# Layer normalisation with a centring product, squares read from PSUM and scaling on VectorE

## What is computed

```python
def _ln_t(v, eps=1e-05):
    m = jnp.mean(v, axis=-1, keepdims=True)
    s = jnp.var(v, axis=-1, keepdims=True)
    return (v - m) / jnp.sqrt(s + eps)
...
x = _L0_conv_ref(x, ...)
t = _to_tokens(x)
t = t + _L1_attn_ref(_ln_t(t), ...)
t = t + _L1_ffn_ref(_ln_t(t), ...)
x = _from_tokens(t, x)
```

## Time and profile before

| What | Value |
|---|---|
| Median of 3 runs | 844.76 us (843.91 to 859.37) |
| The profiled execution: its own time | 852.07 us |
| Its span, first to last instruction | 850.1 us |
| Mean granted TensorE clock | 0.83 |
| Busy: TensorE, VectorE, ScalarE, GpSimd | 688.6, 444.9, 414.2, 132.5 us |
| The attention's normalisation lies at | 513.7 to 540.2 us |
| The experts' normalisation lies at | 783.4 to about 804 us |

### The profile page before, as it was taken

The page is one execution under the profiler, slowest core; times in us unless marked ns, Lnnn a source line. Parts: engine busy times, 40 slices in busy tenths (PEclk is TensorE's granted clock), DMA queues, the critical chain, the costliest instruction groups (busy, mean ns, idle before and its releaser), DMA issues.

```text
span 850.1 us, 42114 instructions
## 1 busy us (share of the span) xinstructions
PE 688.6 (81%) x19610; PEld 502.1 (59%) x19610; DVE 444.9 (52%) x797; ACT 414.2 (49%) x819; POOL 132.5 (16%) x215
## 2 busy tenths in 40 slices
PE   6787777888768789787788675889999999998546
PEld 2355555556552356565566464668888888886333
DVE  0574545445440564545545547246666666664654
ACT  1665554644412665454644414245556665564532
POOL 7000000000003000000000001333444444431400
PEclk8989788876767897778976956559999999999669
DMA  6400000000000400000000005300000000000002
GB/s 179 86 5 4 5 5 5 4 4 5 5 5 5 85 4 5 4 5 5 4 5 5 4 5 123 106 2 2 1 0 0 0 0 0 0 0 2 0 2 99
DMA packets 7691, 16.60 MB, mean 20 GB/s; under 512 B 1837, under 2 KB 5805, under 8 KB 7141
## 3 DMA queue, kind: packets, MB, share of 16 engines
q1 hardware_dynamic: 7534, 14.21, 6.7%
HBM read 10.34 MB, written 3.87 MB: 17 GB/s over the span
## 4 chain that ended last, share of the span: by engine, by line
PE 74%; issue 11%; ACT 6%; DVE 5%; DMA 1%; POOL 1%; SPq 0%; ACTq 0%; DVEq 0%
PE banks L227 21%; PE banks L145 14%; PE banks L716 8%; PE banks L693 4%; PE banks L760 4%; PE banks L458 4%; PE banks L741 4%; PE banks L775 4%; PE banks L180 2%; PE banks L166 2%; ACT hx L273 1%; PE banks L706 1%; ACT hy L278 1%; DVE norm_stats L629 1%; PE banks L729 1%
## 5 line engine op out<-in xcount | busy, mean ns | idle before, releaser
L227 PE MATMUL banks<-s,y 32*64 32x96 f32 (+9 forms) x10752 | 196.1, 271 | 70.8 <-issue 70.5
L318 DVE TENSOR_TENSOR s<-hy,hx 128x384 f32<-128x384 f32 (+3 forms) x336 | 144.6, 476 | 189.1 <-PE banks L227 187.0
L227 PEld LDWEIGHTS banks<-s,y 32*64 32x64 f32 x10752 | 164.0, 157 | 116.2 <-issue 106.3
L145 PE MATMUL banks<-w_dc,tiled 64*32 64x192 f32 x3584 | 128.2, 412 | 19.2 <-issue 12.9
L268 ACT COPY y<-banks 128x384 f32<-128x384 f32 x192 | 81.7, 484 | 108.8 <-PE banks L145 108.6
L145 PEld LDWEIGHTS banks<-w_dc,tiled 64*32 64x32 f32 x3584 | 74.4, 131 | 51.3 <-issue 24.1
L278 ACT ACTIVATE hy<-banks 128x512 f32<-128x512 f32 (+2 forms) x144 | 72.9, 584 | 44.4 <-PE banks L180 44.3
L273 ACT ACTIVATE hx<-banks 128x384 f32<-128x384 f32 x144 | 61.3, 504 | 34.8 <-PE banks L166 28.4
L957 POOL TENSOR_TENSOR y<-y,stats 128x1024 f32<-128x1024 f32 x32 | 60.8, 1901 | 109.3 <-DVE stats L889 109.2
L879 DVE TENSOR_REDUCE stats<-banks 128x16 f32<-128x1024 f32 x32 | 39.2, 1225 | 69.6 <-PE banks L716 69.6
L716 PEld LDWEIGHTS banks<-src,y 64*128 64x128 f32 x1024 | 64.5, 201 | 7.9 <-issue 7.9
(11 more groups left out here) (134 smaller groups left out, 737.4 us busy)
## 6 DMA issues: line engine op xcount, KB each, us to landing
src<-in_x_dram SPq DMA_DIRECT2D x4, 578.0 KB, 5.5
y<-in_w_dram SPq DMA_DIRECT2D x1, 2080.0 KB
off<-in_w_dram SPq DMA_DIRECT2D x2, 1024.0 KB
out_dram<-tokens SPq DMA_DIRECT2D x4, 512.0 KB, 2.6
offsets_dram<-tokens SPq DMA_DIRECT2D x32, 54.0 KB
off<-offsets_dram SPq DMA_DIRECT2D x16, 108.0 KB
w_dc<-in_w_dc_dram SPq DMA_DIRECT2D x2, 288.0 KB, 6.4
y<-in_w_attn_dram SPq DMA_DIRECT2D x1, 512.0 KB, 5.0
```

What stands on the lines that cost most here:

```text
L145: last = nc.tensor.matmul(m.ps[32 * j:32 * j + 32, FIRST_BANK + (count + g) % RING, (col % 2) * 192:(col % 2) * 192 + 192], m.tiled[rows, ...
L227: last = nc.tensor.matmul(out[:, r0:r0 + strip.n, first:first + width], m.y[32 * j:32 * j + 32, g, (s // 3) % 2 * Y_SLOTS + strip.slot, co ...
L318: nc.vector.tensor_tensor(dst, hy, hx[:, :, r0:r0 + strip.n, :], ALU.mult).then_inc(cv.s_ready, 1)
```

## The change

The turn and the centring become one operation. A constant 128 by 128 matrix `centring` (identity less 1/64 within each image's 64 channels) is loaded, and the 8 transpositions of a pair become 8 products with it as the moving operand, so that PSUM holds centred tokens. `centre` on VectorE goes (three instructions a pair). ScalarE squares straight from PSUM. The multiplication moves from GpSimd to VectorE (`scale`), which reads PSUM and writes `xt`; `norm_pool` goes. A product into banks that an earlier pair used now waits for that pair's `scale`. TensorE's program becomes: products 0 and 1, then product 2, back 0, product 3, back 1, back 2, back 3. VectorE's becomes: variance 0 and 1, and then for each pair its invert, its scale and the variance two pairs on. ScalarE's keeps its order.

```diff
+    def centre(pr):
...
         if pr >= 2:
-            pe.wait_ge(ln.centred, pr - 1)
+            pe.wait_ge(ln.scaled, pr - 1)
         for b in range(PIX // P):
-            last = nc.tensor.transpose(m.ps[:, 4 * (pr % 2) + b // 4, b % 4 * P:(b % 4 + 1) * P],
-                                       m.tokens[:, pr, b * P:(b + 1) * P], m.identity[:, :])
-        last.then_inc(ln.turned, 1)
+            last = nc.tensor.matmul(m.ps[:, 4 * (pr % 2) + b // 4, b % 4 * P:(b % 4 + 1) * P],
+                                    m.tokens[:, pr, b * P:(b + 1) * P], m.centring[:, :], start=True, stop=True,
+                                    skip_group_check=True)
+        last.then_inc(ln.centred, 1)
...
+    centre(0)
+    centre(1)
+    for pr in range(PAIRS):
+        if pr + 2 < PAIRS:
+            centre(pr + 2)
+        back(pr)
...
-        nc.scalar.activation(ln.square[:, pr % 2, :, :], ln.xt[pr], ACT.Square).then_inc(ln.squared, 1)
+        nc.scalar.activation(ln.square[:, pr % 2, :, :].rearrange("p b n -> p (b n)"),
+                             m.ps[:, 4 * (pr % 2):4 * (pr % 2) + 2, :].rearrange("p a n -> p (a n)"), ACT.Square
+                             ).then_inc(ln.squared, 1)
...
+    def scale(pr):
+        centred = m.ps[:, 4 * (pr % 2):4 * (pr % 2) + 2, :].rearrange("p a n -> p (a n)").rearrange(
+            "p (b a c) -> p b a c", a=2, c=C)
+        dve.wait_ge(ln.rstd_ready, pr + 1)
+        nc.vector.tensor_tensor(ln.xt[pr].rearrange("p b (a c) -> p b a c", a=2), centred,
+                                over_channels(ln.rstd[:, pr, :]), ALU.mult).then_inc(ln.scaled, 1)
+
+    variance(0)
+    variance(1)
     for pr in range(PAIRS):
-        if pr + 1 < PAIRS:
-            centre(pr + 1)
-        if pr:
-            invert(pr - 1)
-        variance(pr)
-    invert(PAIRS - 1)
+        invert(pr)
+        scale(pr)
+        if pr + 2 < PAIRS:
+            variance(pr + 2)
...
-        pe.wait_ge(ex.ln.centred, 3 + group)
+        pe.wait_ge(ex.ln.scaled, 3 + group)
...
+    c["centring"] = (np.eye(P) - np.kron(np.eye(2), np.ones((C, C))) / C).astype(f32)
```

More of the change, by code:

```diff
@@ L569, in norm_pe @@
 def norm_pe(nc, pe, m, ln, beside):
-    for pr in range(PAIRS):
+    def centre(pr):
         if ("turn", pr) in beside:
@@ L575, in norm_pe, with back @@
         if pr >= 2:
-            pe.wait_ge(ln.centred, pr - 1)
+            pe.wait_ge(ln.scaled, pr - 1)
         for b in range(PIX // P):
-            last = nc.tensor.transpose(m.ps[:, 4 * (pr % 2) + b // 4, b % 4 * P:(b % 4 + 1) * P],
-                                       m.tokens[:, pr, b * P:(b + 1) * P], m.identity[:, :])
-        last.then_inc(ln.turned, 1)
-    for pr in range(PAIRS):
+            last = nc.tensor.matmul(m.ps[:, 4 * (pr % 2) + b // 4, b % 4 * P:(b % 4 + 1) * P],
+                                    m.tokens[:, pr, b * P:(b + 1) * P], m.centring[:, :], start=True, stop=True,
+                                    skip_group_check=True)
+        last.then_inc(ln.centred, 1)
+    def back(pr):
         if ("back", pr) in beside:
@@ L623, in over_channels @@
         return stat.rearrange("p (b a) -> p b a", a=2).unsqueeze(3).to_broadcast([P, PIX // P, 2, C])
[L625 to L636, removed]
     def variance(pr):
@@ L646, in invert @@
         nc.vector.reciprocal(ln.rstd[:, pr, :], ln.rstd[:, pr, :]).then_inc(ln.rstd_ready, 1)
-    centre(0)
-    for pr in range(PAIRS):
-        if pr + 1 < PAIRS:
-            centre(pr + 1)
-        if pr:
-            invert(pr - 1)
-        variance(pr)
-    invert(PAIRS - 1)
[L658 to L663, removed]
+    def scale(pr):
[6 more added lines that the diff above has]
+    variance(1)
+    for pr in range(PAIRS):
+        invert(pr)
+        scale(pr)
+        if pr + 2 < PAIRS:
+            variance(pr + 2)
 TURN_AHEAD, KEYS_AHEAD, SCORES_AHEAD, QUERIES_AHEAD = 1, 2, 3, 4
@@ L1167, in program @@
         m.identity = sb("identity", [P, P])
+        m.centring = sb("centring", [P, P])
         m.tiled = sb("tiled", [P, PAIRS, TR, TC, TILE_ROWS * TILE_COLS])
@@ L1289, in program @@
         ex.ln.xt = [ex.xt[:, :, pr, :] for pr in range(PAIRS)]
-        norm_stats = sb("norm_stats", [P, 3, PAIRS, STATS])
+        norm_stats = sb("norm_stats", [P, 2, PAIRS, STATS])
         for ln in (at.ln, ex.ln):
-            ln.mean, ln.squares, ln.rstd = (norm_stats[:, k, :, :] for k in range(3))
+            ln.squares, ln.rstd = (norm_stats[:, k, :, :] for k in range(2))
             ln.square = s_all[:, 1024:3072].rearrange("p (s b n) -> p s b n", s=2, n=P)
@@ L1296, in program @@
             ln.tokens_before = PAIRS if ln is at.ln else 0
-            ln.turned = sem(name + "_turned")
-            ln.summed = sem(name + "_summed")
-            ln.mean_ready = sem(name + "_mean_ready")
             ln.centred = sem(name + "_centred")
@@ L1391, in program @@
             conv1_loads.append((off_buffer.bitcast(U16)[32 * rg + ROW_COORD:32 * rg + ROW_ONE + 1, :], a["places"][rg]))
-        loads = [(m.identity[:, :], a["identity"]),
+        loads = [(m.identity[:, :], a["identity"]), (m.centring[:, :], a["centring"]),
                  (convs[1].w_off[:, :, :], a["w_off2"]), (convs[1].w_dc[:, :, :], a["w_dc2"]),
@@ L1439, in _ @@
             pool.wait_ge(cleared, PAIRS)
-            norm_pool(nc, pool, m, at.ln)
             attention_pool(nc, pool, m, at)
             pool.wait_ge(at.added, 2 + ALL_BLOCKS)
-            norm_pool(nc, pool, m, ex.ln)
             pool.wait_ge(ex.ln.scaled, PAIRS)
```

## The result

The changed kernel runs in 851.83 us, median of 11 executions (846.47 to 857.75). The kernel before, measured beside it, has 848.96 us (837.25 to 859.37, 11 executions). The ratio is 1.0089, with a 95% interval of 1.0055 to 1.0123: 0.9% slower. Ratios in this document leave out executions more than 1.5% above the fastest of their kernel (here five of the eleven before and none of the changed kernel), and since this program's executions spread that far by themselves, medians over all of them stand beside the ratios. Over all executions the medians differ by 2.9 us and the means (849.6 and 852.4) by 2.8, with a standard error of 2.2 worked out from the 22 times. So the whole times alone say that the change is worth little, and leave its sign open; that has to be read from the stages.

A forecast was written before the change was run, and what follows sets the result against it. It took chains of waits to bound the normalisations, mostly VectorE's sums and subtractions in the experts'. Attention's +1.6 and experts' +4 gave +5.6 us on a median of 844.8, rounded to 851, range 841 to 858.

The forecast's parts named there:

- Twice the records: Centring on TensorE: a pair takes 16 records where there were 8, 1.97 us at the high clock and 3.7 low.
- One chain instead of two pairs in flight: Both normalisations: product 2 waits for scale 0, scale 1 comes after it; 7.55 us per step low clock, 5.82 high.
- two ahead: Engine order: variance and square of pair 2 stand ahead of reciprocal and root of pair 1.
- The rival that the pairs run beside each other: Both normalisations: scale 1 follows scale 0 by VectorE's 2.7 us a pair, saving some 5 us each; 835 us; 3%.
- Scale 0: First pair's multiplication, now on VectorE: ends at 523.95 in the attention's normalisation and 791.6 in the experts'.
- early lead over GpSimd's multiplication: Attention's normalisation: scale 0 ends at 523.95 instead of 527.8 on GpSimd, 3.8 us ahead, given back afterwards.
- +1.6 forecast: Attention's normalisation: 1.6 us longer, taken as the middle between low and high clock throughout.
- the ends of -0.8 and +4.0: Attention's normalisation: 0.8 us earlier with the high clock throughout, 4.0 us later with the low clock throughout.
- +3 forecast for the chain: Experts' normalisation: first gate product 3 us later, between 0.8 at the high clock and 5.1 at the low.
- The further +1 for the gate products: After the experts' normalisation: 1 us more, since at the low level the gate products' 1.89 us become up to 3.8.
- The rival of a clock held high through the opening: Normalisations and attention's opening: centring bursts keep the clock high, sum -5 us, 840 us; 14%.
- the prediction's third sign of being wrong: Attention's opening: the prediction is wrong if it runs at another clock than before.

The follow-up runs named there:

- experiment with turns: Changed kernel with the 8 centring products of a pair made transpositions with the identity again, mean not subtracted; median 846.62 us against 846.27 before, ratio 1.0003.
- second changed execution: The changed kernel profiled once more without any edit; 844.93 us in a single execution, beside 855.05 us for the kernel before.
- own banks: Changed kernel with two PSUM banks for each of the four pairs and all four products first on TensorE; ratios to the kernel before 0.9793 and 0.9805.

## Why the prediction was right

**The time.** 851 was forecast, 851.83 measured, in the range, and the direction was forecast too (5.6 us slower; the ratio says 0.9%, some 7.5 us; the medians differ by 2.9; the two stages by 5.3). That the forecast hit the median so closely is luck: the median of before was given as 844.76 from three executions and is 848.96 over the 11 here, and 844.8 + 5.6 is 850.4, which "rounded to 851" puts too high. What the profiles and the experiments bear out is the sum over the stages.

**Twice the records.** 128 records for 64, and 3.75 and 2.02 us for a pair at the two clocks, for 3.7 and 1.97 forecast. The experiment with turns prices this on the chain at 7.0 us for both stages, where 5 to 7 was expected.

**One chain instead of two pairs in flight.** This was the step on which the sign rested, since it is the opposite of what "two ahead" suggests. From the end of one scale to the end of the next, 7.22 and 7.53 us in the attention's stage and 7.63 and 5.90 in the experts' stage were measured, for 7.55 (low clock) and 5.82 (high clock) forecast. The second changed execution has 6.50 and 5.90, and 7.62 and 6.48, by the scales' starts. Moving the order on both engines closed the pairs up, on VectorE alone it didn't, and own banks removed the wait altogether. The rival that the pairs run beside each other is out for this kernel and right for those.

**Scale 0.** It ended 10.2 us after the start of the attention's stage (10.9 in the second execution), forecast 10.3, and 8.1 (in both) after the start of the experts' stage, forecast 8.2. The early lead over GpSimd's multiplication was real, and the chain gave it back.

**The stages.** Attention's: +1.6 forecast, +2.2 measured; both executions lay between the ends of -0.8 and +4.0. Experts' stage: +3 forecast for the chain, +3.1 measured. The further +1 for the gate products was not borne out: the first group took 2.37 us in one changed execution (1.94 in the other) and in the two of before 1.89 and 2.57, so they vary alike in both kernels. Without it the forecast is 4.6 us, for 5.3 measured.

**The clock.** The rival of a clock held high through the opening came true in one profiled execution of two, and the kernel before ran low there in both. An opening at another clock was also the prediction's third sign of being wrong, and the first changed execution shows it; the second, with 30.5 us as before, shows that the chain doesn't hang on it. The two short openings over all versions, 23.2 and 23.3 us, both stand among the eight profiles with centring products and none among the five with turns; two of eight are too few to tie them to the change. The prediction also read the kernel before too simply: between the rise near 517 and the fall near 527 lies a dip, with the granted clock at 0.53 in 520 to 522 and 0.62 in 522 to 524.

Over the normalisations themselves the granted clock differs too. In the attention's it averaged 0.59 to 0.71 in the five profiles with turns and 0.71 to 0.89 in the eight with products; in the experts', 0.61 to 0.74 and 0.78 to 0.93. The changed kernel has 0.76 and 0.74, and 0.80 and 0.78; the same kernel with turns in the place of products 0.59 and 0.71. So part of what the second record costs may come back through the clock; no run separates that part. The Trainium skill's rule ("TensorE: Matmul & The Clock Gate", Part 4: PE-mode transpose), that transposing doesn't bring the full clock, does not hold here as it stands: before, the clock rose behind turns alone, and at the start of the attention's stage it rose in three of the five profiles with turns. That products bring it sooner than turns agrees with these figures, but a pair's products also keep TensorE busy for twice as long, and nothing here tells the two apart. What stays open is how the clock falls out in a given execution.

**What else stays open.** Own banks save 11.9 us in the two stages against before, while the medians differ by 13.6 and 18.7. Two profiles don't show where the remainder comes from, and the convolutions alone spread by 15.6 us.

## What to carry to other kernels

A stage count such as "two ahead" means nothing until one has followed, for the second item, every queue that it passes and every buffer that it needs. Here PSUM banks held until the last consumer turned a wait for an early step into a wait for the whole chain, and two in-order queues with the third item ahead of the second made sure of it. When work is moved from one engine to another and the buffer's last reader changes, look at who wants the buffer next; if there is room, give each item its own, and only then judge the arithmetic: the centring product costs 7 us on the chain and, by an estimate, 2 to 3 us off it. And where executions of one kernel spread over 15 us and more, cut the profile into stages and compare the stages.

## What the runs showed of the hardware that was not expected

The attention's opening, the same instructions in every version, took 30.5 us in seven of the thirteen profiled executions, about 29.6 in four, and 23.2 or 23.3 in two, at a granted clock of 0.50, 0.54 and 0.83. TensorE's busy time goes with it (25.9, 24.7 and 16.4 us), while VectorE's is 12.2 us in all. The stretch before the first turn, some 500 us of two unchanged convolutions, took from 498.1 to 513.7 us. The attention's blocks took 212.3 to 213.5 us in ten profiles and 216.8 to 217.0 in three, at a clock of 0.99 to 1.00 and of 0.98.

In the first 6 us of the attention's stage, the granted clock averaged 0.55 to 0.74 in all eight profiled executions with centring products: it rose from the low level during their burst. With turns there it rose in three of five (0.75, 0.67, 0.64) and stayed at 0.50 in two, so that there the head products ran at the low level. These are too few profiles to say how much of the difference is more than chance.
